# Six edits in the transformer stack: gelu, the variance's reciprocal root, and the order of the seeds on ScalarE

## The reference, cut to what matters

```
q, k, v = split(x @ Wqkv)               # 16 heads of 64
q, k = l2norm(q) * qs, l2norm(k) * ks   # then rotary
x = local_attention(q, k, v) @ Wo + x   # windows of 32 rows, softmax
mu  = x.mean(-1);  var = ((x - mu) ** 2).mean(-1)
xn  = (x - mu) / sqrt(var + 1e-05) * g + bln
a, gate = split(xn @ W1 + b1)
x = a * gelu(gate) @ W2 + b2 + x
```

## Time and profile before

| what | value |
|---|---|
| median of 3 runs | 4276.08 us |
| the profiled execution's own time | 4277.94 us |
| its span, first to last instruction | 4276.2 us |
| TensorE matmul busy | 3789.2 us, 89% |
| VectorE | 3357.8 us, 79% |
| ScalarE | 2526.5 us, 59% |
| GpSimd | 2501.7 us, 59% |
| mean granted TensorE clock | 0.971 of full speed |

### The profile page before, as it was taken

The page is one execution under the profiler, slowest core; times in us unless marked ns, Lnnn a source line. Parts: engine busy times, 40 slices in busy tenths (PEclk is TensorE's granted clock), DMA queues, the critical chain, the costliest instruction groups (busy, mean ns, idle before and its releaser), DMA issues. The chain is left out here.

```text
span 4276.2 us, 153902 instructions
## 1 busy us (share of the span) xinstructions
PE 3789.2 (89%) x67640; PEld 2277.3 (53%) x67640; DVE 3357.8 (79%) x4385; ACT 2526.5 (59%) x3236; POOL 2501.7 (59%) x2036
## 2 busy tenths in 40 slices
PE   6887799999999999999678886899999999999996
PEld 3232456666666666666333333566666666666664
DVE  7998788888888888888354436788888888888884
ACT  5886456666666666666223453566566665666664
POOL 0001677777787777876100005787777877777772
PEclk8999999999999999999789998999999999999998
DMA  0001232323323223222000002323323233232221
GB/s 20 1 1 42 67 87 67 91 72 79 89 67 91 73 78 90 64 70 62 17 1 1 1 1 78 90 74 85 78 73 89 73 84 80 74 88 71 69 63 40
DMA packets 165604, 260.98 MB, mean 61 GB/s; under 512 B 58574, under 2 KB 79818, under 8 KB 164938
## 3 DMA queue, kind: packets, MB, share of 16 engines
q1 hardware_dynamic: 164936, 251.13, 22.5%
HBM read 48.61 MB, written 1.05 MB: 12 GB/s over the span
## 5 line engine op out<-in xcount | busy, mean ns | idle before, releaser
L1382 POOL TENSOR_TENSOR f_k_rotated<-f_rope_ak,f_rope_bk 128x1024 f32<-128x1024 f32 x192 | 454.1, 2365 | 271.6 <-DVE f_rope_bk L1432 271.6
L1098 PE MATMUL banks<-f_wqkv,H 128*128 128x512 f32 x1152 | 561.7, 611 | 23.2 <-DVE f_rope_bk L1432 12.2
L1098 PE MATMUL banks<-f_wqkv,G 128*128 128x512 f32 x1152 | 552.9, 602 | 1.0 <-issue 1.0
L1364 POOL MEMSET f_kT<- 128x256 f32 x2 | 0.6, 312 | 840.5 <-POOLq L514 461.1
L1382 POOL TENSOR_TENSOR f_q_rotated<-f_rope_aq,f_rope_bq 128x1024 f32<-128x1024 f32 x192 | 454.9, 2369 | 52.9 <-DVE f_rope_bq L1432 52.6
L1155 PEld LDWEIGHTS banks<-f_O_T,f_wo 128*128 128x128 f32 x3072 | 372.5, 192 | 106.0 <-issue 93.2
L1322 ACT ACTIVATE f_V<-banks 128x1024 f32<-128x1024 f32 x192 | 196.0, 1021 | 377.6 <-PE banks L1098 377.6
L1155 PE MATMUL banks<-f_O_T,f_wo 128*128 128x128 f32 x3072 | 375.4, 275 | 11.0 <-issue 8.4
L1429 DVE TENSOR_TENSOR f_rope_aq<-banks,f_rope 128x1024 f32<-128x1024 f32 x192 | 235.0, 1224 | 184.7 <-ACT f_sqq L1287 169.2
L1394 POOL TENSOR_TENSOR f_q_rotated<-f_q_rotated,f_inverse_norm 128x1024 f32<-128x1024 f32 x192 | 365.5, 1903 | 15.0
L1376 POOL TENSOR_TENSOR f_E<-f_E,f_row_inverse 128x1024 f32<-128x1024 f32 x192 | 367.9, 1916 | 8.0 <-DVE f_row_inverse L1464 8.0
(11 more groups left out here) (207 smaller groups left out, 9075.0 us busy)
## 6 DMA issues: line engine op xcount, KB each, us to landing
f_P_T_paired<-f_P_T SPq DMA_DIRECT2D x1536, 64.0 KB, 2.0
f_V_previous<-f_V SPq DMA_DIRECT2D x192, 384.0 KB, 3.9
f_V_previous<-f_V SPq DMA_DIRECT2D x192, 128.0 KB, 2.5
f_wqkv<-in_L_ffn_Wqkv SPq DMA_DIRECT2D x48, 384.0 KB, 3.7
f_rope<-in_rope SPq DMA_DIRECT2D x24, 512.0 KB, 4.2
f_wo<-in_L_ffn_Wo SPq DMA_DIRECT2D x12, 512.0 KB, 5.5
f_w<-in_L_ffn_W SPq DMA_DIRECT2D x12, 341.0 KB
f_w<-in_L_ffn_W SPq DMA_DIRECT2D x24, 64.0 KB
```

The source lines that it names most:

```text
L1098: mm = nc.tensor.matmul(ps[:, o * BLK:(o + 1) * BLK], xs, w[:, c * INNER + o * BLK:c * INNER + (o + 1) * BLK], start=True, stop=True)
L1382: nc.gpsimd.tensor_tensor(qk[i][:], ra[i][:], rb[i][:], ALU.add).then_inc(radd.sem, 1)
```

## The change

Six edits, all in the stack.

1. Slot 3, ScalarE: the gelu moves behind the copy of V. The table load for it is written out and stays ahead of the copy of V; the load of the other table follows the gelu.
2. ScalarE, every slot: the seeds of the reciprocal norms (Ln, Exp) move ahead of the exponential of E.
3. VectorE adds epsilon and multiplies by -0.5 in the one instruction of line 1497; ScalarE's Ln then scales by -2.
4. ScalarE squares the seed (one more instruction of 128x512 at the end of slot 0).
5. GpSimd keeps one product of the four: square times (-0.5 (var + eps)).
6. VectorE scales xn by the seed (the old instruction of line 1504 with another operand) and then by (product + 1.5) in a second fused instruction.

```diff
-                if (b := feed(s, 11)) is not None:
-                    act.wait_ge(f_gev.sem, f_gev.at(blk(b)))
-                    nc.scalar.activation(ge[:].rearrange("p j t -> p (j t)"), ge[:].rearrange("p j t -> p (j t)"),
-                                         ACT.Gelu).then_inc(f_ge.sem, 1)
+                if feed(s, 11) is not None:
+                    nc.scalar.preload_act_table_set("gelu_and_others")
                 if live(s):
                     act.wait_ge(v_mm.sem, v_mm.at(n))
                     act.wait_ge(o_mm.sem, o_mm.past(n - 4))
                     act.wait_ge(vp_in[n % 3].sem, vp_in[n % 3].past((n - 3) // 3))
                     nc.scalar.activation(V[n % 4][:], PV_F, ACT.Copy).then_inc(v_ev.sem, 1)
-                if feed(s, 11) is not None:
+                if (b := feed(s, 11)) is not None:
+                    act.wait_ge(f_gev.sem, f_gev.at(blk(b)))
+                    nc.scalar.activation(ge[:].rearrange("p j t -> p (j t)"), ge[:].rearrange("p j t -> p (j t)"),
+                                         ACT.Gelu).then_inc(f_ge.sem, 1)
                     nc.scalar.preload_act_table_set("natural_log_exp_and_others")
...
-                if live(s - 1):
-                    act.wait_ge(sbd.sem, sbd.at(n - 1))
-                    nc.scalar.activation(E[(n - 1) % 2][:], E[(n - 1) % 2][:], ACT.Exp).then_inc(expd.sem, 1)
                 if live(s):
                     act.wait_ge(clamped.sem, clamped.at(n))
                     act.wait_ge(newton.sem, newton.past(n - 1))
                     nc.scalar.activation(lg[:], ss[n % 2][:], ACT.Ln).then_inc(seeded.sem, 1)
                     act.wait_ge(seeded.sem, seeded.at(n, 1))
                     nc.scalar.activation(y0[:], lg[:], ACT.Exp, scale=-0.5).then_inc(seeded.sem, 1)
+                if live(s - 1):
+                    act.wait_ge(sbd.sem, sbd.at(n - 1))
+                    nc.scalar.activation(E[(n - 1) % 2][:], E[(n - 1) % 2][:], ACT.Exp).then_inc(expd.sem, 1)
                 if (b := feed(s, 8)) is not None:
...
-                    nc.scalar.activation(xsq[:], var[:], ACT.Ln).then_inc(f_seed.sem, 1)
+                    nc.scalar.activation(xsq[:], var[:], ACT.Ln, scale=-2.0).then_inc(f_seed.sem, 1)
                     act.wait_ge(f_seed.sem, f_seed.at(blk(b), 1))
+                    act.wait_ge(f_xn.sem, f_xn.past(blk(b) - 1))
                     nc.scalar.activation(vy0[:], xsq[:], ACT.Exp, scale=-0.5).then_inc(f_seed.sem, 1)
+                    act.wait_ge(f_seed.sem, f_seed.at(blk(b), 2))
+                    nc.scalar.activation(xsq[:], vy0[:], ACT.Square).then_inc(f_seed.sem, 1)
...
                     pool.wait_ge(f_seed.sem, f_seed.at(blk(b)))
-                    nc.gpsimd.tensor_tensor(xsq[:], vy0[:], vy0[:], ALU.mult).then_inc(f_nt.sem, 1)
-                    pool.wait_ge(f_nt.sem, f_nt.at(blk(b), 1))
-                    nc.gpsimd.tensor_tensor(xsq[:], xsq[:], var[:], ALU.mult).then_inc(f_nt.sem, 1)
-                    pool.wait_ge(f_nt.sem, f_nt.at(blk(b), 2))
-                    nc.gpsimd.tensor_scalar(xsq[:], xsq[:], -0.5, 1.5, ALU.mult, ALU.add).then_inc(f_nt.sem, 1)
-                    pool.wait_ge(f_nt.sem, f_nt.at(blk(b), 3))
-                    nc.gpsimd.tensor_tensor(var[:], xsq[:], vy0[:], ALU.mult).then_inc(f_nt.sem, 1)
+                    pool.wait_ge(f_xn.sem, f_xn.past(blk(b) - 1))
+                    nc.gpsimd.tensor_tensor(var[:], xsq[:], var[:], ALU.mult).then_inc(f_nt.sem, 1)
...
-                    nc.vector.tensor_scalar(var[:], bank(5), EPS, None, ALU.add).then_inc(f_eps.sem, 1)
+                    nc.vector.tensor_scalar(var[:], bank(5), EPS, -0.5, ALU.add, ALU.mult).then_inc(f_eps.sem, 1)
...
-                    nc.vector.scalar_tensor_tensor(xn[:], xcs[:], vec[b // NBLK % 2][:, 0:1], var[:], ALU.mult, ALU.mult)\
+                    nc.vector.scalar_tensor_tensor(xn[:], xcs[:], vec[b // NBLK % 2][:, 0:1], vy0[:], ALU.mult, ALU.mult)\
                         .then_inc(f_xn.sem, 1)
+                    dve.wait_ge(f_xn.sem, f_xn.at(blk(b), 1))
+                    nc.vector.scalar_tensor_tensor(xn[:], var[:], 1.5, xn[:], ALU.add, ALU.mult).then_inc(f_xn.sem, 1)
```

More of the change, by code:

```diff
@@ L931, in ffn_stack @@
         f_xc, f_sq, f_xcs, f_var, f_eps, f_seed = sig("x_centered"), sig("x_squared"), sig("x_centered_copied"), \
-            sig("var_done"), sig("eps_added"), sig("var_seeded", 2)
-        f_nt, f_xn, f_xb = sig("var_newton_steps", 4), sig("xn_scaled"), sig("xn_ready")
+            sig("var_done"), sig("eps_added"), sig("var_seeded", 3)
+        f_nt, f_xn, f_xb = sig("var_newton_steps"), sig("xn_scaled", 2), sig("xn_ready")
         f_g, f_gev, f_ge, f_a, f_hm = sig("gate_done", 3), sig("gate_evacuated", 3), sig("gelu_done"), \
@@ L1495, in _ @@
                     dve.wait_ge(f_var.sem, f_var.at(blk(b)))
-                    dve.wait_ge(f_nt.sem, f_nt.past(blk(b) - 1))
-                    nc.vector.tensor_scalar(var[:], bank(5), EPS, None, ALU.add).then_inc(f_eps.sem, 1)
+                    dve.wait_ge(f_xn.sem, f_xn.past(blk(b) - 1))
+                    nc.vector.tensor_scalar(var[:], bank(5), EPS, -0.5, ALU.add, ALU.mult).then_inc(f_eps.sem, 1)
                 if (b := feed(s, 9)) is not None:
```

## The result

The changed kernel takes 4287.2 us (median of 20 runs, 4278.7 to 4295.9), the kernel before 4278.2 us (20 runs, 4270.4 to 4289.2). The ratio is 1.0018, its 95% interval 1.0011 to 1.0025. The forecast was 4283, range 4241 to 4298, and "the same": both hold, and the time went where case A put it.

The account below looks back on a forecast made before the run. TensorE was taken to bound the kernel, idle mostly where transposes wait for GpSimd. Slots 0 and 1 (+7 us), slot 3 (+9) and the drains (-8.6) gave +7, so 4283 us against the median, range 4241 to 4298.

Parts of the forecast that it names:

- case A: GpSimd's small instruction in slot 1 is held and ScalarE's square eats slot 0's gain: 4283 us, chance 0.44.
- Slot 3, gelu and exponential: ScalarE's seeds come 0.24 us later: moving gelu costs 1.19, moving the exponential gives 0.95; +9 us over 36 slots.
- Slot 0, seeds against square: Earlier seeds cover TensorE's 0.27 us idle, but ScalarE's extra square delays the scores: +0.06 us per slot.
- Slot 1, the port: VectorE's second scaling holds GpSimd's last small instruction: q normalised 0.1 us later instead of 0.31 earlier.
- Rival B: In slot 1 GpSimd's small instruction slips through without being held: 4263 us, chance 0.25.
- Drain: After each stack's last live slot, shorter chains on GpSimd and VectorE save 4.3 us per stack, 8.6 in all.
- Sum: Slots 0 and 1 +7 us over 44 groups, slot 3 +9, drains -8.6: +7 us in all.
- C: Neither ScalarE's square nor gelu's move is felt; slot 0 gives 0.27 us, slot 1 0.35: 4240 us, chance 0.18.
- My line of 100: Sign that the forecast is wrong and C holds: TensorE's waits for GpSimd fall below 100 us in all.
- D: In slot 1 GpSimd's normalisation of q gets the port ahead of the second scaling: +70 us, 4350 us, chance 0.06.
- E: In slot 0 ScalarE's later queue delays the scores by 0.3 us instead of 0.06: 4294 to 4300 us, chance 0.05.
- F: In slot 3 automatic table loads double the written-out ones, 1.28 us each, 46 times: 4340 us, chance 0.02.

Follow-up runs that it names:

- the kernel with both repairs: The changed kernel with the gelu ahead of the copy of V again and the seed's square back on GpSimd: 4222.3 us, ratio 0.9869 to the kernel before.
- the experiment: The changed kernel with VectorE's second scaling moved behind the new state, ahead of the addition to the state, in slot 1: 4300.0 us, ratio 1.0045.

## Why the prediction was right, point by point

The medians over slots 8 to 94 of each stack answer each step of the sum. In sum over the same slots of the two profiled executions, slot 0 changed by +0.3 us, slot 1 by +7.5, slots 2 and 3 by +6.5.

| slot | before | after | difference | forecast |
|---|---|---|---|---|
| 0 | 16.35 | 16.26 | -0.09 | +0.06 |
| 1 | 17.03 | 17.10 | +0.07 | +0.10 |
| 2 and 3 | 16.23 + 16.55 | 16.11 + 16.93 | +0.26 | +0.24 |
| drains | 92.3 + 84.2 | 86.4 + 81.6 | -8.5 | -8.6 |

- **Slot 3, gelu and exponential**: right to 0.02. The slot's own length grew by 0.38, but the copy of V starts 0.12 earlier with nothing in front of it, so slot 2 is shorter by that. The idle before the transposes of q has a median of 0.55; I had written 0.75, because the slot of the earlier trace rows has 0.53 where the median before is 0.35. The rise, 0.20, is near the one forecast. Counted from the load in 42 slots, the transposes of k start 0.19 later in the mean and the next copy of V 0.31 later, 13 us for the forecast's 9.
- **Slot 0, seeds against square**: the mechanism is right in every part, the balance has the other sign. Squares of q 0.59 later (0.65), last copy of kT ends 0.45 later (0.5), rotation of k starts 0.35 later (0.4), no wait for k, and a wait of ScalarE's in its place. The balance came out at -0.09 where I had +0.06, because the transposes of k start 0.39 earlier in the slot and not 0.27.
- **Slot 1, the port**: right, and the step that decided between A and B. Ln starts 0.35 earlier (0.31), two small instructions are held instead of one, and the normalisation of q starts 0.08 later (0.1). Without the second scaling the slot takes 0.42 less. Rival B, GpSimd slipping through, is excluded: its request came 0.12 or 0.13 behind VectorE's in 43 of 44 slots.
- **Drain**: the sum is right, the shares are not, so its closeness is in part luck. It is -5.9 for the first stack and -2.6 for the second, where I had -4.3 each.
- **Sum**: the slots give 44 x 0.24 = +10.6 and the live parts +15.2, where I had +16; summed and not by medians the slots give +14.3. That the total agrees to 2 us is luck: TensorE's gaps without a shown cause differ by 7 us between the two traces, as much as the whole forecast.
- **Rivals**: C, that the gains come through, fell on the time and on the waits, 139.9 us in all. My line of 100 was badly set, though: the kernel with both repairs, faster than C's 4240, still has 111.5. D did not come, as VectorE asked before GpSimd's last small instruction. Its price of 70 us is not measured: D has the request at the start of q's normalisation, and in the experiment it fell 1.5 us into it (median), for a cost of 13. D was too dear at TensorE all the same: it moves the transposes of k as far as those of q, and in the experiment q's came 0.76 later and k's 0.02. E did not come: slot 0 got shorter. F did not either: two loads per slot 3, as before.
- **The rule weighed**: the Trainium skill ("SBUF — State Buffer", section "SBUF: two separate sides") has the loser blocked for the whole instruction of the other. The trace agrees in both directions: on GpSimd 0.25 became 0.68, and on VectorE a scaling of 0.69 took up to 2.34, when it was asked for 0.11 us behind the start of k's normalisation. What the page does not settle, who is next when the holder has another instruction queued, the experiment showed: the one that waits.

The change is thus several gains and three losses on the same waits. Two of the losses, the gelu's place and ScalarE's square, can be left out whole (40 and 25 us), and the third, the hold in slot 1, nearly so (10 us, which is not clear of noise): the fastest kernel is the changed one without them.

## What to carry to other kernels

In front of an engine that works in order, ask for each instruction whether what stands behind it is late already: the same gelu cost 0.2 us while ScalarE waited for TensorE's projection, and 26 to 40 us in all one place further back. Work moved off an engine that is not the last pays only if it goes to one with room at that moment, and a long VectorE instruction with two SBUF inputs beside a chain of short GpSimd ones held two of them here, 0.22 to 0.60 and 0.25 to 0.68. Put it where GpSimd does something that nothing waits for.

## What the runs showed that I had not expected

The port goes to the engine that waits when the holder's instruction ends, even with the holder's next instruction queued: in 38 slots the late scaling waited for the rest of one normalisation and GpSimd's next took 2.35 instead of 1.90, and in the 4 where it was asked for during that next one, it waited for that one's end.

TensorE's clock fell more often where a kernel added idle time: with 0.95 us more of it per slot 3, the granted clock was at its lower level in 15 of 42 of them, against 2 of 42 before and 1 after, and each such slot took 1.6 us more.

Third, in every kernel here TensorE has 82 to 108 gaps of 60 to 78 us in all that no semaphore explains (100 gaps, 74.8 us before; 95, 67.6 after). Many fall in other slots each time, but not all: the slots 10, 26, 42, 58 and 74 of each stack hold 11 to 23 us of them in every kernel (18.5 before, 12.8 after), nearly all in front of the values. Sync issues the loads of the next layer's scales (lines 1004 to 1006) for the slot ahead of each; that this is the cause isn't shown. Timeline of the kernel before, TensorE:

```profile
3031.50 0.24 PE L1132 MATMUL banks<-f_V_previous,f_P_T_paired 64*32 64x64 f32 x2 [3.14 <-issue]
```

The clock often falls there too, in 3 of the ten slots before and 4 after, and their summed length goes from 170 to 198 us over the eleven kernels. That is as large as the effects of single edits, so a sum of 44 equal slots can't be more exact than some 10 us.
